# Biases moved off TensorE, a deeper expert pipeline and another order at the end of a transformer layer with routed experts

## The reference, cut to what matters

```python
# x: 4 batches x 512 tokens x 256
Q, K, V = relu(x@Wq.T + bq), relu(x@Wk.T + bk), x@Wv.T + bv     # 16 heads of 16
Q, K = Q * decay, K * decay
KV = einsum('bhnd,bhne->bhde', K, V);  Ksum = K.sum(tokens)
out = (Q @ KV) / (Q . Ksum + 1e-6)
x = layernorm(x + out @ Wo.T + bo)
p = softmax(x @ w_gate); two best of 8 experts per token, weights renormalised
routed = sum over both of weight * (silu(x@G_e) * (x@U_e)) @ D_e      # inner width 128
shared = (silu(x@G) * (x@U)) @ D                                     # inner width 512
x = layernorm(x + routed + shared)
```

## Time and profile before

| | |
|---|---|
| median of three runs | 256.34 us |
| the profiled execution's own time | 257.67 us |
| its span | 255.7 us |
| busy: TensorE, VectorE, ScalarE, GpSimd | 90%, 60%, 45%, 54% |
| chain that ended last | TensorE 62%, VectorE 18%, DMA 6%, no cause shown 5%, GpSimd 3% |
| granted TensorE clock, mean | 0.97 of full |

### The profile page before, as it was taken

How to read it: one execution, slowest core, us unless ns; L and a number is a source line. 1 busy time by engine, 2 the same in 40 slices (tenths; PEclk the granted TensorE clock), 3 DMA queues, 4 the chain that set the end, 5 groups by cost and what they waited for, 6 DMA issues and landing times.

```text
span 255.7 us, 5039 instructions
## 1 busy us (share of the span) xinstructions
PE 231.2 (90%) x1440; PEld 197.1 (77%) x1440; DVE 152.4 (60%) x526; ACT 115.9 (45%) x298; POOL 137.3 (54%) x161
## 2 busy tenths in 40 slices
PE   8989989989989999999993999999999989994960
PEld 2458888788879788789991988888888878893960
DVE  2783363276546959669645466666666624999521
ACT  2262613832570731752603466666666644324600
POOL 0072486899688888656582066555555560030420
PEclk9999999999999999999998699999999999998896
DMA  5943038321441121222532255455555305952222
GB/s 167 368 161 103 3 101 311 86 66 39 110 137 62 44 84 41 85 83 103 174 135 70 82 146 157 140 151 160 154 167 144 118 19 155 342 163 82 75 91 82
DMA packets 21579, 31.72 MB, mean 124 GB/s; under 512 B 3248, under 2 KB 14257, under 8 KB 21556
## 3 DMA queue, kind: packets, MB, share of 16 engines
q1 hardware_dynamic: 17552, 22.46, 29.3%
q0 software_dynamic: 3456, 8.43, 9.5%
q10 hardware_dynamic: 548, 0.53, 0.6%
HBM read 19.70 MB, written 12.76 MB: 127 GB/s over the span
## 4 chain that ended last, share of the span: by engine, by line
PE 62%; DVE 18%; DMA 6%; issue 5%; POOL 3%; ACT 3%; SPq 1%; POOLq 0%; DVEq 0%; ACTq 0%
PE bank L329 17%; PE bank L331 13%; PE bank L330 13%; PE bank L598 4%; POOL x_slots L1325 3%; DVE x L1209 3%; PE bank L371 3%; DMA x_slots<-x,slot 3%; DMA k_sb<-in_batt 2%; PE bank L435 2%; PE bank L619 2%; PE bank L475 2%; PE bank L385 2%; DVE xt_raw L1021 2%; DVE wa_lo L904 2%
## 5 line engine op out<-in xcount | busy, mean ns | idle before, releaser
L1369 POOL DMA_INDIRECT y_pairs<-x_t,dst x40 | 38.9, 973 | 36.5 <-DVE dst L1167 30.1
L329 PE MATMUL bank<-wf_hi,ot_hi 128*128 x120 | 42.2, 352 | 1.5 <-issue 1.0
L1325 POOL DMA_INDIRECT x_slots<-x,slot x32 | 31.9, 998 | 14.7 <-issue 8.3
L330 PE MATMUL bank<-wf_lo,ot_hi 128*128 x120 | 34.7, 289 | 0.0
L331 PE MATMUL bank<-wf_hi,ot_lo 128*128 x120 | 34.6, 289 | 0.0
L329 PEld LDWEIGHTS bank<-wf_hi,ot_hi 128*128 128x128 f32 x120 | 23.5, 196 | 8.2 <-issue 7.2
L329 PE MATMUL bank<-x1t_hi,wf_hi 128*128 128x512 f32 x64 | 26.0, 406 | 0.5 <-DVE xt_raw L1021 0.5
L331 PE MATMUL bank<-x1t_hi,wf_lo 128*128 128x512 f32 x64 | 25.3, 395 | 0.0
L330 PE MATMUL bank<-x1t_lo,wf_hi 128*128 128x512 f32 x64 | 25.2, 394 | 0.0
L1306 POOL TENSOR_TENSOR wf_lo<-stage,wf_hi 128x512 fp32r<-128x512 f32 x18 | 23.1, 1286 | 1.5
L330 PEld LDWEIGHTS bank<-wf_lo,ot_hi 128*128 128x128 f32 x120 | 23.7, 197 | 0.0
(11 more groups left out here) (175 smaller groups left out, 622.9 us busy)
## 6 DMA issues: line engine op xcount, KB each, us to landing
o_sb<-x_slots SPq DMA_DIRECT2D x40, 129.0 KB, 2.1
stage<-in_wffn SPq DMA_DIRECT2D x18, 256.0 KB, 2.7
x<-in_x SPq DMA_DIRECT2D x4, 512.0 KB, 6.6
out<-x SPq DMA_DIRECT2D x8, 256.0 KB, 2.1
xt_raw<-in_xT SPq DMA_DIRECT2D x3, 512.0 KB, 6.1
x_slots<-fill SPq DMA_DIRECT2D x9, 129.0 KB, 2.8
x<-in_watt SPq DMA_DIRECT2D x4, 256.0 KB, 6.1
k_sb<-y_pairs SPq DMA_DIRECT2D x2, 512.0 KB, 4.4
```

Source lines behind the costliest of these rows:

```text
L329: mm(o, w_hi, m_hi, start=start, stop=False, **more)
L330: mm(o, w_hi, m_lo, start=False, stop=False, **more)
L1325: pool.indirect_dma_start(out=x_scat, out_offset=bass.IndirectOffsetOnAxis(ap=slot[:, j, t:t + 1], axis=0), in_=x1[:, t, :], in_offset=Non ...
L1369: pool.indirect_dma_start(out=y_scat, out_offset=bass.IndirectOffsetOnAxis(ap=dst[:, j:j + 1], axis=0), in_=ey[:, u, :], in_offset=None, b ...
```

## The change

Six edits go together.

1. Key, value and output bias. The value bias leaves the projection: VectorE adds `bv * Ksum` to KV in `kvm_out`. The output bias leaves `proj_o`: VectorE adds it to the residual rows of two batches at a time, in iterations 0 and 1, between `o_out(b, 1)` and `o_out(b, 2)`. The key bias stays on TensorE, with 256 instead of 512 columns. Two more DMAs on ScalarE's queue bring both rows to all 128 partitions.
2. Output projection. The transposes go half by half (m outside t), `proj_o` begins the first two row tiles with the first half.
3. `bf_ready` is waited for in `ranks(0)`, not before the first `k_t_v`.
4. GpSimd's list is written out anew: chunks 0 to 3 ahead of `split_x_lo(2)`, 13 chunks by `x1_lo(0)`, and a wait `landed(0, 1)` ahead of `scatter(1, 0)`.
5. Experts. Tiles are turned three steps ahead, over four banks and four buffers of `xe_hi`/`xe_lo`; the turned h and the result have one bank each, with a wait for their last reader.
6. End. `last_rows` of all four tiles come before `shared_dn(3, ...)`, over four banks; moments, factors and norm go by tiles 0 and 1, 2, 3.

```diff
@@ proj_kv @@
-                    split3(o, xt_hi[:, b % 2, k, c], xt_lo[:, b % 2, k, c], wa_hi[:, w], wa_lo[:, w], k == 0, False)
-                mm(o, one_f[:, :], b_row[:, 0:2 * D], start=False, stop=True).then_inc(S["kv_mm"], 1)
+                    last = split3(o, xt_hi[:, b % 2, k, c], xt_lo[:, b % 2, k, c], wa_hi[:, w], wa_lo[:, w],
+                                  k == 0, k == KD - 1)
+                    if k == 0:
+                        mm(o[:, 0:D], one_f[:, :], b_row[:, 0:D], start=False, stop=False)
+                last.then_inc(S["kv_mm"], 1)
@@ o_transposed, proj_o @@
-                for t in range(TB):
-                    pe.wait_ge(S["o_out"], TB * b + t + 1)
-                    for m in range(KD):
+                for m in range(KD):
+                    for t in range(TB):
+                        if m == 0:
+                            pe.wait_ge(S["o_out"], TB * b + t + 1)
...
-                    mm(o, one_f[:, :], b_row[:, 2 * D:3 * D], start=True, stop=False)
...
+                for k in range(KD):
+                    pe.wait_ge(S["ot_hi_out"], KD * b + k + 1)
+                    pe.wait_ge(S["ot_lo_out"], KD * b + k + 1)
+                    for t in (0, 1):
+                        last = product(t, k)
+                        if k == KD - 1:
+                            last.then_inc(S["y_mm"], 1)
+                for t in (2, 3):
+                    pe.wait_ge(S["r_out"], TB * b + t - 1)
+                    product(t, 0)
+                    product(t, 1).then_inc(S["y_mm"], 1)
@@ experts on TensorE @@
+                if j >= 1:
+                    pe.wait_ge(S["he_lo_out"], j)
+                nc.tensor.transpose(h_bank[:, 0:P], eh[:, u % 2, :], ident).then_inc(S["eht_mm"], 1)
...
+                if j >= 1:
+                    pe.wait_ge(S["ey_out"], j)
+                split3(y_bank[:, 0:D], he_hi[:, u % 2, :], he_lo[:, u % 2, :],
...
-                    e_transposed(s + 2, v, i + 2)
+                    if s + 3 < NT:
+                        e_transposed(s + 3, (v + 1) % RING, i + 2 + (v + 1) // RING)
@@ end on TensorE @@
             shared_dn(2, 1)
+            for t in range(TB):
+                last_rows(t)
             shared_dn(3, 0)
             shared_dn(3, 1)
@@ ScalarE's queue @@
+            act.dma_start(bv[:, :], batt[0:1, D:2 * D].broadcast_to([P, D])).then_inc(S["bvo_in"], 16)
+            act.dma_start(bo, batt[0:1, 2 * D:3 * D].broadcast_to([P, D])).then_inc(S["bvo_in"], 16)
@@ VectorE @@
-                v.tensor_tensor(kvm[:, :, 0:P], o[:, :, 0:P], blk.unsqueeze(1).broadcast_to([P, KD, P]), ALU.mult)
+                for m in range(KD):
+                    ins = v.scalar_tensor_tensor(kvm[:, m, 0:P], bv[:, m * P:(m + 1) * P], o[:, m, P:P + 1],
+                                                 o[:, m, 0:P], ALU.mult, ALU.add)
+                link(ins)
+                v.tensor_tensor(kvm[:, :, 0:P], kvm[:, :, 0:P], blk.unsqueeze(1).broadcast_to([P, KD, P]), ALU.mult)
...
+            def residual_bias(b):
+                dve.wait_ge(S[f"res_in{b}"], 16)
+                r = x1[:, b * TB:(b + 1) * TB, 0:D]
+                v.tensor_tensor(r, r, bo.unsqueeze(1).broadcast_to([P, TB, D]), ALU.add).then_inc(S["bo_out"], 1)
...
                     o_out(b, t)
+                    if b < 2 and t == 1:
+                        residual_bias(2 * b)
+                        residual_bias(2 * b + 1)
...
-            for h in range(TB // 2):
-                last_moments(3, range(2 * h, 2 * h + 2))
-            for t in range(TB):
+            last_moments(3, range(0, 2))
+            last_moments(3, range(2, 3))
+            for t in range(0, 2):
+                apply_norm(NB - 1, t)
+            last_moments(3, range(3, 4))
+            for t in range(2, TB):
                 apply_norm(NB - 1, t)
@@ GpSimd @@
+            for i in range(0, 4):
+                split_chunk(i)
+            split_x_lo(2)
+            for i in range(4, 7):
+                split_chunk(i)
+            x1_norm(0)
+            for i in range(7, 11):
+                split_chunk(i)
+            split_x_lo(3)
+            for i in range(11, 13):
+                split_chunk(i)
+            x1_lo(0)
+            x1_norm(1)
+            for i in range(13, NCH):
+                split_chunk(i)
+            scatter(0, 0)
+            x1_lo(1)
+            x1_norm(2)
+            scatter(0, 1)
+            landed(0, 1)
             scatter(1, 0)
```

More of the change, by code:

```diff
@@ L137, in build @@
         te_i = sb("te_i", [1, WORDS], I32)
-        b_raw = k_sb[:, 0:3, :].rearrange("p a d -> p (a d)")
+        b_raw = k_sb[:, 0, :]
+        bo = hot[:, :, :].rearrange("p j n -> p (j n)")
         fill = sb("fill", [P, DT])
@@ L468, in shared_gu, with last_rows @@
                     last.then_inc(S["sgu_mm"], 1)
-            def last_rows(o, t):
+            def last_rows(t):
                 i = T - TB + t
+                o = last_sum(t)
+                if t == 2:
+                    pe.wait_ge(S["sh_out"], NB * CS - 1)
                 pe.wait_ge(pair_in[i // UNIT], 16)
@@ L493, in shared_dn @@
                                       c == 0 and b < NB - 1, c == CS - 1)
[L494 removed]
+                    if b == NB - 1 or t % 2:
+                        last.then_inc(S["sdn_mm"], 1)
             def first_kv():
@@ L842, in _ @@
             e_x_hi(1, 1)
+            e_x_hi(2, 2)
             e_silu(0, 0)
-            e_x_hi(2, 2)
+            e_x_hi(3, 3)
             e_silu(1, 1)
             e_h_hi(0, 0)
-            e_x_hi(3, 3)
+            e_x_hi(4, 0)
             e_silu(2, 2)
@@ L852, in _ @@
             for s in range(2, 2 + RING - 1):
-                e_x_hi(s + 2, (s + 2) % RING)
+                e_x_hi(s + 3, (s + 3) % RING)
                 e_silu(s + 1, (s + 1) % RING)
@@ L859, in _ @@
                     s = i * RING + (v + RING + 1)
-                    e_x_hi(s + 2, (v + 3) % RING)
+                    e_x_hi(s + 3, v)
                     e_silu(s + 1, (v + 2) % RING)
@@ L1184, in _ @@
             e_x_lo(1, 1)
+            e_x_lo(2, 2)
             e_h(0, 0)
-            e_x_lo(2, 2)
+            e_x_lo(3, 3)
             e_h(1, 1)
             e_h_lo(0, 0)
-            e_x_lo(3, 3)
+            e_x_lo(4, 0)
             e_h(2, 2)
             e_h_lo(1, 1)
-            with dve.Fori(0, NT // RING - 1) as i:
+            with dve.Fori(0, NT // RING - 2) as i:
                 for w in range(RING):
                     s = i * RING + (w + 2)
-                    e_x_lo(s + 2, w)
+                    e_x_lo(s + 3, (w + 1) % RING)
                     e_h(s + 1, (w + 3) % RING)
                     e_h_lo(s, (w + 2) % RING)
-            e_h(NT - 1, (NT - 1) % RING)
-            for s in (NT - 2, NT - 1):
+            for s in range(NT - RING - 2, NT):
+                if s + 3 < NT:
+                    e_x_lo(s + 3, (s + 3) % RING)
+                if s + 1 < NT:
+                    e_h(s + 1, (s + 1) % RING)
                 e_h_lo(s, s % RING)
@@ L1330, in landed @@
                 pool.wait_ge(S[f"scattered{b}"], 16 * TOPK * (TB // 2) * (part + 1))
-            per = -(-NCH // (NB - 1))
             split_x_lo(1)
-            done = 0
-            for b in range(NB - 1):
-                for n in range(per):
-                    if b == 2 and n == 4:
-                        scatter(0, 0)
-                        x1_lo(b - 1)
-                        x1_norm(2)
-                    split_chunk(done)
-                    done += 1
-                    if b == 2 and n == 4:
-                        scatter(0, 1)
-                    if n == 1 and b + 2 < NB:
-                        split_x_lo(b + 2)
-                    if n == 5 and b == 0:
-                        x1_norm(0)
-                    if n == 3 and b == 1:
-                        x1_lo(b - 1)
-                        x1_norm(1)
+            for i in range(0, 4):
[18 more added lines that the diff above has]
+            landed(0, 1)
             scatter(1, 0)
@@ L1380, in _ @@
             b = NB - 1
-            for h in range(TB // 2):
-                ts = slice(2 * h, 2 * h + 2)
-                pool.wait_ge(S["bn_out"], b * TB + 2 * h + 2)
+            for ts in (slice(0, 2), slice(2, 3), slice(3, 4)):
+                pool.wait_ge(S["bn_out"], b * TB + ts.stop)
                 link(g.tensor_scalar(nw[:, b, 0, ts], mv[:, b, ts, 1], EPS_LN, None, ALU.add))
```

102 lines of the change are left out of this document (48 added, 54 removed).

## The result

The changed kernel takes **253.25 us** (median of four runs, 252.40 to 253.98) against 256.19 us for the kernel before, run beside it (255.49 to 257.27): a ratio of 0.988, 95% interval 0.983 to 0.993. It is faster, by 1.2% or 3 us; I had forecast 243.6 us, with 240.5 as the low end and 248.5 as the high. The profiled execution took 253.98 us, with a span of 252.2; that of the kernel before took 257.67, with a span of 255.7.

The account below looks back on a forecast made before the run. The prediction took TensorE, busy nearly everywhere but for four places of waiting, to bound the kernel. Attention 3.1, expert steps 4.7 and end 4.9 us, together 12.7, off 256.34 gave 243.6 us, range 240.5 to 248.5.

Parts of the forecast that it names:

- Attention: Start and batches 0 to 3, up to batch 3's moments: 3.1 us gained.
- The start: Ahead of the batches: no wait for `tri`, shorter bias matmuls, less 0.3 for added DMAs; 1.2 us gained.
- From there to the experts: From batch 3's moments to the first expert tile: GpSimd's list runs earlier, experts start 3.1 us sooner (1.5 to 4.6).
- the clash in batch 3: Batch 3's attention: VectorE's `hot` operations held up beside GpSimd's splitting; this would go, 1.1 us gained.
- My rival of VectorE eating the gain: Attention: residual adds at 5 us a pair, mask held up; gain 0.1 instead of 3.1, time 246.6 us; chance 0.09.
- The experts' start: First expert tile: its split stands behind VectorE's `diag` tiles, which move by 3.1 us; start counted 3.1 us sooner.
- The experts: Expert loop: earlier splits remove a gap, 36 steps fall from 1.64 to 1.51 us; 4.7 us gained (0 to 4.7).
- if TensorE's own issue makes them: Expert steps: gaps come from TensorE's issue or ScalarE's order, steps stay 1.64, time 248.3 us; chance 0.12.
- The end: Last row tiles, factors and norm: TensorE's pause at 231 us goes; 4.9 us gained (4.0 to 5.3).
- my case: Whole kernel: all gains come, the granted clock still falls in the pause before the experts; 243.6 us, chance 0.61.
- the first rival: Before the experts: the clock stays up, first steps run at full rate, some 2.1 us more, 241.5 us; chance 0.15.
- The sum: Whole kernel: 3.1 + 4.7 + 4.9 = 12.7 us off the median of 256.34, giving 243.6 us.

Follow-up runs that it names:

- a3: The changed kernel without the adds of the output bias to the residual rows, so that bias is missing from the result: 249.96 us, ratio 0.972.
- a9: The changed kernel itself, unaltered, run again beside a kernel before that takes 264.00 us there: 269.74 us, ratio 1.022.
- a4: The changed kernel with fixed expert numbers in place of those read from te_i (result not the layer's): 245.83 us, ratio 0.954.
- a5: The changed kernel with the next word of expert numbers loaded one step sooner, behind the third step's gate-up: 253.19 us, ratio 0.986.

## Why the prediction was wrong

**Attention: right at the size, wrong at the place.** The start came 1.34 us earlier (1.2 said) and the parts give 3.05 at batch 3's moments (3.1 said), with the old list; the 0.8 us between equal traces leave some luck in so close a match. With the new list batch 3 lost it.

**The step that failed first** is in "From there to the experts": "In the new list I place its operations one behind the other with their old durations ... so it is about 6 us early at `scatter(1, 0)`". GpSimd was 1.0 us early there (91.39 against 92.40), and ahead of that it was late; without the adds, in a3, it was 5.5 us early (86.87), as I had placed it. After has `scatter(0, 0)` at 74.71 (before: 73.67), and batch 2's factors, which I never followed to batch 3's rows, at 82.39 (81.31). Two things were missing. The durations are not the old ones: VectorE's adds lengthen the chunks beside them by 3.3 us, and I had costed that clash on VectorE alone. And the loads are not free: chunk 6 stands behind the residual and x loads on SyncE's queue, 2.51 us. From 18 us to `scatter(0, 0)` the new list saves 9.3 us of waiting for ScalarE (8.20 and 1.11) and pays 3.9 for two more chunks, 2.9 for loads (7.3 instead of 4.5) and 3.3 beside the adds: 0.8 us more, where `scatter(0, 0)` is 1.0 later. I had placed the adds in a pause of VectorE and the chunks in a pause of GpSimd without seeing that it is the same moment. Of the clash in batch 3 the part on attention says "so it goes"; it moved to the cast of `ix_f`, 2.52 us. My rival of VectorE eating the gain had each pair of adds at 5.0 us and the mask held up; the pairs took 2.78 and 3.44, and the mask 0.42 in batch 3. The price lay on GpSimd. The price of the list with the adds: 101.15 - 96.17 = 5.0 us at the moments (3.4 by a9's), 1.5% in the ratios (0.988 and 0.973).

**The experts' start.** T(0) came at 138.47 (138.37 before), its gate-up at 142.89: VectorE made the `diag` tiles until 142.07 and only then the split. I had named that order and given it no time.

**The experts: 4.7 us said, 1.8 measured.** The gap of 0.24 us ahead of a gate-up was for the greater part not the split's: of the 0.22 us by which a step of 1.64 is longer than a4's 1.42, the older split took 0.05 and fixed numbers the other 0.17. These 6.0 us hang on the expert numbers, and the change leaves them. That was in the main a rival of mine, at 0.12, "if TensorE's own issue makes them". The tail took 1.0 us of the 1.8 back.

**The end: right**, 5.2 us for 4.9. No pause at 231, clock 1.00 behind it, factors in three rounds with waits of 1.04 and 0.56.

**The clock** came out between my case and the first rival. It stayed at 1.00 from 134.5 to 139.5 because batch 3's late products filled that stretch, and fell to 0.50 behind the next pause; TensorE ran at half clock there for about 3.4 us, before for about 6.8 (worked out from the means of each us).

**The sum** by what was measured: attention with its list +2.8, made up to +2.5 at the gate-up, clock and first steps -0.5, 36 steps -1.8, tail and shared products +1.0, end -5.2: -4.0 at the last norm, -3.5 in the span. My range left out a list that is late, and so all of the 5 us. Its inner ends are also a little off their own terms: 4.6 + 4.7 + 5.3 gives 241.7 and not 240.9, 1.5 + 3.6 + 4.9 gives 246.3 and not 246.5; neither matters for the miss.

**For use:** of the versions with the right result, the best measured is a1, the change with GpSimd's old order: 0.973 (0.965 to 0.981), against 0.988 (0.983 to 0.993) for the change; the intervals do not meet, though each is from a group of its own. It was not run where the kernel before takes 262 us.

## What to carry to other kernels

When work is moved on VectorE and on GpSimd at once, lay the two timelines over each other at the new times: an operation that is free in the other engine's pause is paid twice when both fill the same pause, and the payer can be the engine that you did not look at. Follow each moved operation to what its last result releases two stages on (here factors, apply, transpose), not only to its neighbour. And before taking a gap without a releaser as a wait for data, look for what the queue itself must do there: fixed numbers in place of loaded ones are a cheap test.

## What the runs showed of the hardware

- A cast of 128 x 8 on VectorE took 2.52 us in after, across two GpSimd subtractions back to back: it got in neither before nor between them. In a4, a5 and a9 it took 1.70, in a3, beside a scatter, 0.17.
- Reading expert numbers on TensorE's queue and addressing weights by registers cost 0.17 us on a step of 1.42 (after and a4), also when the load stood behind a running gate-up (a5).
- Two VectorE adds of 128 x 1024 from SBUF took 2.35 us in a GpSimd pause (a1); beside GpSimd's splits they took 2.78 and 3.44, and GpSimd lost 3.3 us (after against a3).
- The same two kernels stood at 0.988 and at 1.022 to each other, where the kernel before takes 256 and 264 us; on one chip the kernel before took 258 and, some minutes later, 262.
